# A two-layer network with two recurrences and two mixtures of experts: the first mixture taken out of the first recurrence

## What is computed

```python
x = x + linear_attention(local_attention(x, cond))      # 16 heads of 64
x = x + ffn0(gru(cond, x))
x = x + diff_attention(gated_recurrence(cond, x))
x = x + ffn1(modulate(x, cond))
```

```python
def step(h, inp):                      # h is [8, 128]
    r = sigmoid(xr_t + h @ W_hr)
    z = sigmoid(xz_t + h @ W_hz)
    n = tanh(xn_t + r * (h @ W_hn + b_hn))
    return (1.0 - z) * n + z * h
```

```python
for e in range(8):
    y = relu(tokens @ W1[e] + b1[e]) @ W2[e] + b2[e]     # 128 -> 512 -> 128
    out = out + where(final_e == e, y, 0.0)
```

## Time and profile before

| | us |
|---|---|
| median of three runs | 1699.1 (1698.83 to 1703.48) |
| the profiled execution | 1703.39, its span 1701.6 |
| PE busy | 1564.6 (92% of the span), 11861 passes |
| DVE, ACT, POOL busy | 827.5, 662.9, 94.7 |

### The profile page before, as it was taken

One profiled execution on the slowest core, in us unless ns is written; L12 is line 12 of the kernel. 1 busy time (PEld: TensorE's weight loads), 2 busy tenths in 40 slices (PEclk: granted clock), 3 DMA queues, 4 the chain that ended last, 5 costly groups with the idle time before them and its releaser, 6 DMA issues. The chain is left out here.

```text
span 1701.6 us, 32009 instructions
## 1 busy us (share of the span) xinstructions
PE 1564.6 (92%) x11861; PEld 1250.0 (73%) x11862; DVE 827.5 (49%) x2926; ACT 662.9 (39%) x2449; POOL 94.7 (6%) x135
## 2 busy tenths in 40 slices
PE   7999989879999899999999999879999999866995
PEld 5666555537777799999999999638888888753663
DVE  2777668755445334444444444473333333565223
ACT  3211112125555145555555455314344434523442
POOL 0000000000000000000000000010000000003662
PEclk9988889889999999999999999859999999967998
DMA  4000000000000300000000000010000000001113
GB/s 146 1 1 1 0 1 1 1 0 1 1 1 1 100 1 2 2 1 2 2 2 1 2 2 1 1 31 21 20 26 20 27 14 2 1 1 47 41 43 92
DMA packets 27731, 28.05 MB, mean 16 GB/s; under 512 B 2293, under 2 KB 22234, under 8 KB 27450
## 3 DMA queue, kind: packets, MB, share of 16 engines
q1 hardware_dynamic: 20970, 16.70, 3.4%
q0 software_dynamic: 2496, 5.12, 1.0%
q10 hardware_dynamic: 4112, 4.19, 0.8%
HBM read 21.35 MB, written 4.65 MB: 15 GB/s over the span
## 5 line engine op out<-in xcount | busy, mean ns | idle before, releaser
L1457 PE MATMUL spare<-identb 128*128 128x128 bf16 x3166 | 218.2, 219 | 0.0
L1457 PEld LDWEIGHTS spare<-identb 128*128 128x128 bf16 x3166 | 201.7, 103 | 4.3
L292 PE MATMUL sc<-headsel,prod 128*128 128x128 f32 x1024 | 164.6, 315 | 0.7 <-DVE prod L437 0.7
L292 PEld LDWEIGHTS sc<-headsel,prod 128*128 128x128 f32 x1024 | 142.6, 218 | 26.7 <-issue 24.3
L1055 DVE TENSOR_TENSOR_SCAN narg<-rz,pre_n 128x16 f32<-128x16 f32 x256 | 47.9, 187 | 219.9 <-PE pre_n L952 218.9
L990 ACT ACTIVATE ghid<-gh_ps,cols 128x128 f32<-128x128 f32 x512 | 144.3, 366 | 12.9 <-PE gh_ps L891 12.7
L891 PE MATMUL gh_ps<-hist,w 128*128 128x128 f32 x1024 | 137.5, 275 | 0.6 <-ACT ghid L990 0.6
L900 PE MATMUL gy_ps<-w2e,ghid 128*128 128x128 f32 x1024 | 136.8, 276 | 0.6
L900 PEld LDWEIGHTS gy_ps<-w2e,ghid 128*128 128x128 f32 x1024 | 124.4, 191 | 3.0 <-issue 3.0
L891 PEld LDWEIGHTS gh_ps<-hist,w 128*128 128x128 f32 x1024 | 126.0, 188 | 0.8 <-DVE hist L1063 0.8
L952 PE MATMUL pre_r<-hist,gru_w 128*128 128x128 f32 x512 | 118.1, 312 | 0.7 <-DVE hist L1063 0.5
(11 more groups left out here) (374 smaller groups left out, 2664.1 us busy)
## 6 DMA issues: line engine op xcount, KB each, us to landing
w<-in_L_ffn_W SPq DMA_DIRECT2D x1, 2048.0 KB, 9.6
raw<-in_L_ffn_wg SPq DMA_DIRECT2D x8, 256.0 KB, 2.9
raw<-in_L_ffn_wu SPq DMA_DIRECT2D x8, 256.0 KB, 2.8
raw<-in_L_ffn_wd SPq DMA_DIRECT2D x8, 256.0 KB, 2.7
wqkv<-in_L_attn_Wqkv SPq DMA_DIRECT2D x1, 1536.0 KB, 6.4
mrow<-mt SPq DMA_DIRECT2D x4, 256.0 KB, 2.4
y_top<-yrow SPq DMA_DIRECT2D x4, 256.0 KB, 5.4
y_next<-yrow ACTq DMA_DIRECT2D x4, 256.0 KB, 6.1
```

Source lines behind the costliest of these rows:

```text
L292: mm = nc.tensor.matmul(sc[:, :, :, :].rearrange("p i j h -> p (i j h)"), prod[u % 2][:, j, P * i:P * i + P], headsel[:, P - 2 * k:2 * P - ...
L1457: nc.tensor.matmul(spare[:, 0:P], n.identb[:, :], n.identb[:, :], start=True, stop=True)
```

## The change

In gru_scan the mixture's jobs, diff, y0, choice and the hist clearing go. The three products of a step stream the eight columns of the state. At step 3 of a group PE turns the group's 128 states (one transposition), ACT copies them to htok, and SP stores them as rows of a DRAM tensor hrow. Fills stand in every step: 12, or 8 where input products are fed, and both now come behind them. b1 and b2 are loaded to all partitions by SP. In route_top1 the diagonal and the adding go; chosen and kept stay for a new stage, sparse_ffn: final expert (one), places and lists as in sparse_experts with 16 pair columns and 24 block columns, then 23 slots, each with a gather, one hidden product, and bias adds on VectorE; rows are scattered to frow, read back in four parts by SP, turned, and added to xT.

```diff
-    FILL = 16
+    FILL = 12
+    INPUT_FILL = 8
+    RING = 4
...
+                sp.dma_start(b1B[:, :], a["L0_ffn_b1"].rearrange("(r e) f -> r (e f)", r=1).broadcast_to([P, E * FF])).then_inc(n.load_experts, 16)
+                sp.dma_start(b2B[:, :], a["L0_ffn_b2"].rearrange("(r e) d -> r (e d)", r=1).broadcast_to([P, E * D])).then_inc(n.load_experts, 16)
+                for g in range(GROUPS):
+                    sp.wait_ge(h_kept, g + 1)
+                    sp.dma_start(hrow[P * g:P * g + P, :], htok[g % RING][:, :]).then_inc(h_stored[g % RING], 16)
...
-            @block.gpsimd
-            def _(pool):
-                pool.memset(hist[:, 16 * 40:], 0.0).then_inc(hist_zero, 1)
...
+                for s in range(T):
+                    h = second(at_step(s))
+                    pe.wait_ge(state, s + 1)
+                    for out, i, ready in ((gate_slot(pre_r, s), 3, r_pre), (first(n_slot(s)), 5, n_pre), (gate_slot(pre_z, s), 4, z_pre)):
+                        nc.tensor.matmul(out, n.gru_w[:, i, :], h, start=False, stop=True,
+                                         skip_group_check=True).then_inc(ready, 1)
+                    if s >= G and s % G == TURN_AT:
+                        turn(s // G - 1)
                     g, i = s // G + 1, s % G - 9
-                    if g < GROUPS and 0 <= i < 7:
+                    feeds = g < GROUPS and 0 <= i < 7
+                    if feeds:
                         inputs(g, i)
+                    for _ in range(INPUT_FILL if feeds else FILL):
+                        nc.tensor.matmul(spare[:, :], n.identb[:, :], n.identb[:, :], start=True, stop=True)
+                pe.wait_ge(state, T + 1)
+                turn(GROUPS - 1)
+                for k in range(NBLK):
+                    b, half = divmod(k, SEG)
+                    states = hist[:, 16:16 * (T + 1)].rearrange("p (t b two) -> p two b t", b=B, two=2)[:, 1]
+                    mm = nc.tensor.matmul(pre_r[0][:, E * k:E * k + E], states[:, b, P * half:P * half + P],
+                                          n.cols[:, r0:r0 + E], start=True, stop=True)
+                mm.then_inc(all_logits, 1)
...
+def sparse_ffn(nc, n, chosen, kept, hrow, frow, w1, w2, b1B, b2B):
+
+    SLOTS = (TOK + E * (P - 1)) // P
+    COLS = 24
+    AHEAD = 8
+    RING = 10
+    YRING = 4
...
+                def hidden(j):
+                    if j >= SLOTS:
+                        return
+                    at[j] = pe.value_load(owner_i[0:1, j:j + 1], min_val=0, max_val=E - 1)
+                    pe.wait_ge(x_kept, j + 1)
+                    if j >= 2:
+                        pe.wait_ge(hid_done, j - 1)
+                    nc.tensor.matmul(h_ps[j % 2][:, :], xT[j % 3][:, :],
+                                     w1[:, bass.ds(at[j], 1), :].rearrange("p e f -> p (e f)"),
+                                     start=True, stop=True).then_inc(h_in, 1)
...
+                def down(j):
+                    pe.wait_ge(t_kept, j + 1)
+                    if j >= 1:
+                        pe.wait_ge(y_kept, j)
...
+                for j in range(SLOTS):
+                    hidden(j + 1)
+                    turn_in(j + 2)
+                    turn_hidden(j)
+                    if j >= 1:
+                        down(j - 1)
+                down(SLOTS - 1)
+                pe.wait_ge(t_kept, SLOTS)
+                for g in range(4):
+                    pe.wait_ge(f_back[g], 16)
...
+                for j in range(SLOTS):
+                    keep_in(j + 2)
+                    act.wait_ge(t_in, j + 1)
...
+                    nc.scalar.activation(hidT[j % 2][:, :, :], t_ps[j % 2][:, :, :], ACT.Relu).then_inc(t_kept, 1)
...
+                def add(j):
...
+                    own[j] = dve.value_load(owner_i[0:1, j:j + 1], min_val=0, max_val=E - 1)
+                    dve.wait_ge(h_in, j + 1)
+                    if j >= 2:
+                        dve.wait_ge(t_in, j - 1)
+                    V.tensor_tensor(hid[j % 2][:, :], h_ps[j % 2][:, :], b1B[:, bass.ds(own[j] * FF, FF)], ALU.add).then_inc(hid_done, 1)
+
+                def keep_out(j):
+                    dve.wait_ge(y_in, j + 1)
+                    if j >= YRING:
+                        dve.wait_ge(scattered[j % YRING], 16 * (j // YRING))
+                    V.tensor_tensor(ysb[j % YRING][:, :], y_ps[:, :], b2B[:, bass.ds(own[j] * D, D)], ALU.add).then_inc(y_kept, 1)
...
+                for j in range(SLOTS):
+                    gather(j + AHEAD)
+                    pool.wait_ge(y_kept, j + 1)
+                    pool.indirect_dma_start(out=frow[:, :],
...
+                for g in range(4):
+                    sp.dma_start(back[:, 4 * g:4 * g + 4, :],
+                                 frow[512 * g:512 * g + 512, :].rearrange("(i p) d -> p i d", p=P)).then_inc(f_back[g], 16)
```

More of the change, by code:

```diff
@@ L884, in inputs @@
                     nc.tensor.matmul(out, lhsT, rhs, start=(i < 3), stop=False, skip_group_check=True)
[L886 to L932, removed]
-                    if k == 7 and g < GROUPS:
-                        pe.wait_ge(choice_kept, g + 1)
-                        nc.tensor.matmul(turn_ps, n.b2[:, :], choiceT[:, :], start=True, stop=True).then_inc(bias_in, 1)
@@ L1119, in route_top1 @@
         counts = sb("r_counts", [P, 3, NBLK])
-        rank, kept = sb("r_rank", [P, NBLK]), sb("r_kept", [P, NBLK])
-        diag = sb("r_diag", [P, NBLK, P], BF16)
-        added = [sb(f"r_added{i}", [P, 2 * T]) for i in range(4)]
+        rank = sb("r_rank", [P, NBLK])
         const = sem("r_const"); step = sem("r_step")
@@ L1304, in _ @@
             def _(pe):
[L1305 to L1315 removed]
+                pe.wait_ge(const, 2)
@@ new lines, in _ @@
+                pe.wait_ge(taken_done, 1)
+                nc.tensor.matmul(tot_ps, ones[:, :], taken[:, :, :], start=True, stop=True)
+                nc.tensor.matmul(cum_ps, tri[:, :], taken[:, :, :], start=True, stop=True).then_inc(counted, 1)
+                pe.wait_ge(pay_done, 2)
+                for q in range(NBLK):
+                    if q % 8 == 0:
+                        pe.wait_ge(lane_done, q // 8 + 1)
+                    mm = nc.tensor.matmul(inv_ps[:, :], in_lane[:, q, :], load[:, q, :, :].rearrange("p k c -> p (k c)"),
+                                          start=(q == 0), stop=(q == NBLK - 1), skip_group_check=True)
@@ new lines, in _ @@
+                at = {}
+                pe.wait_ge(owners, 1)
+                turn_in(0)
+                turn_in(1)
+                hidden(0)
+                for j in range(SLOTS):
+                    hidden(j + 1)
+                    turn_in(j + 2)
+                    turn_hidden(j)
+                    if j >= 1:
+                        down(j - 1)
[3 more added lines that the diff above has]
+                    pe.wait_ge(f_back[g], 16)
+                    if g >= 2:
+                        pe.wait_ge(added, g - 1)
+                    for i in range(4):
+                        mm = nc.tensor.transpose(t_ps[g % 2][:, i, :], back[:, 4 * g + i, :], n.ident[:, :])
+                    mm.then_inc(turned, 1)
@@ new lines, in done, with after, per_token @@
+                def done(ins):
+                    at[0] += 1
+                    ins.then_inc(step, 1)
+                def after():
+                    dve.wait_ge(step, at[0])
+                def per_token(ap):
+                    return ap.unsqueeze(2).broadcast_to(wide)
+                done(V.tensor_scalar(dropped[:, :], kept[:, :], -1.0, 1.0, ALU.mult, ALU.add))
+                done(V.tensor_tensor(one[:, :, :], chosen[:, :, :], per_token(kept[:, :]), ALU.mult))
+                after()
@@ new lines, in _ @@
+                dve.wait_ge(blk_done, 1)
+                V.tensor_tensor(load[:, :, 1, :], in_blk[:, :, :], pair_no[:, :].unsqueeze(2).broadcast_to(every),
+                                ALU.mult).then_inc(pay_done, 1)
+                for c in range(2):
+                    eight = [P, 8, P]
+                    V.tensor_tensor(in_lane[:, 8 * c:8 * c + 8, :], lane[:, :].unsqueeze(1).broadcast_to(eight),
+                                    lo_f[:, 8 * c:8 * c + 8].unsqueeze(2).broadcast_to(eight), ALU.is_equal).then_inc(lane_done, 1)
```

434 lines of the change are left out of this document (259 added, 175 removed).

## The result

The changed kernel takes 1940.8 us (median of 4 runs, 1937.7 to 1952.3), the kernel before 1699.0 beside it: ratio 1.144, 95% interval 1.138 to 1.150. The forecast was 1690. The profiled execution has a span of 1939.0 us and a mean granted clock of 0.779, against 1701.6 and 0.942 before.

What follows compares the result with a forecast made beforehand. It took the state-to-state chain to bound steps without extras, TensorE's queue the others. Terms -3.4, -65.5, -17.4 and +77 (new stage) sum to -9.3 us: 1703.4 profiled to 1694.1, as median 1690; own range 1681 to 1699.

Steps and rivals of the forecast that it cites:

- rival 3: Recurrence: with fewer columns streamed the clock falls, 2.7 us a step at the lower level, 1715 to 1780 us; chance 0.05.
- recurrence: First recurrence, 256 steps: falls from 485.7 to 420.2 us, -65.5 us, mean step 1.65 us.
- Narrow products: Recurrence steps without extras: eight columns instead of 128 take 0.11 us off, 1.72 to 1.61 us.
- Rival 1: Recurrence: narrow products save less; 0.05 us instead of 0.11 gives 1705 us, nothing gives 1718; chance 0.16.
- bias steps: Recurrence steps 12 to 15 of a group, feeding a one-row bias: bound by TensorE's queue at 1.76 us.
- Start: Before the recurrence: hist memsets and two VectorE constants go, products start earlier; -3.4 us.
- Behind the recurrence: Between recurrence and ranking: mixture jobs and router products shrink to 32 router passes, 26.1 to 8.7 us, -17.4 us.
- Lists: Beginning of the new stage: building the lists on VectorE up to the first gather takes 13.0 us.
- filling: New stage after the lists: first gather to first hidden product takes 5.0 us.
- Slots: New stage, 23 slots: each takes 2.30 us, with GpSimd's 2.58 us a transfer pair covered by gathering eight ahead.
- Rival 2: New stage: slots stall as TensorE waits for the copied output; 3.16 us a slot gives 1709 us; chance 0.16.
- The last part: End of the new stage, after the last output product: read-back, transposes, last add and block change, 12.0 us.

Runs made afterwards that it cites:

- e18: Changed kernel with only the middle product (n) streaming 128 columns again, fills 12 and 8, one-row biases; 1694.1 us (ratio 0.9976).
- e2: Changed kernel with fills where input products are fed raised from 8 to 12, so all steps have twelve; 1991.7 us (ratio 1.168).
- e7: Kernel before the change with its three products narrowed from 128 to 8 columns, mixture jobs and sixteen fills kept; 2086.8 us (ratio 1.228).
- e11: e9 with one pause: in step 64 VectorE first fills a tile of 8192 columns; 1953.7 us, a single run.
- e9: Changed kernel with fifteen and twelve fills and biases fed by weights of 128 rows instead of one; 1695.6 us (ratio 0.9973).
- e6: Changed kernel with fills raised to twenty, and sixteen in steps 9 to 15; 2145.1 us (ratio 1.253).
- e10: e9 with all 23 gathers issued ahead of the first scatter, 23 input and 12 output buffers; 1707.3 us (ratio 1.004).

## Why the prediction was wrong

- **The clock, rival 3 at 0.05.** This is the step that failed: the sum took the full clock for the whole recurrence. Its term was 420.2 us, and 656.7 was measured, 236.5 of the 250.8 us between forecast and median. Against the rival stood: "Against it: the second recurrence, eight columns with fourteen fills a step, ran at 0.99". The comparison was made per step. A step of the second recurrence lasts 1.19 us and has one product, so fourteen fills in 1.19 us; here twelve stand in 1.60 us beside six passes of eight columns, where six passes of 128 columns stood before. That this difference of the two steps is the reason is argued and not shown, since no run varies it alone; what is shown is that the same fills hold the clock when one of the three products is wide (e18). The rival's price per step, 2.7 us, was right (42.1 / 16 = 2.63 measured); that the fall would be for the whole recurrence was not in its prices, 1715 to 1780, since I took it for granted that the clock comes back. The kernel after itself, e2, e7 and e11 show that it does not. The row quoted for a falling clock, "two stretches with idle TensorE at 0.50", has one stretch at 0.50 in the earlier trace rows; the ranking, which is not among these rows, has 0.54.
- **Narrow products, -0.11 us a step.** Right: 1.60 measured, 1.61 forecast. Rival 1 is out. The bias steps were priced too high, 1.76 for 1.60 in step 12: the one-row load starts 0.77 us into the step and not 0.84 (591.48 against 590.71), the fills' loads come 0.41 later, as priced, and the next product's load 0.42 behind their start, not 0.45 and 0.05. A single weight load of 0.19, from which the six passes were priced, is not in the earlier trace rows, which show the pair alone; loads of this length stand elsewhere in the trace. Where the clock holds, the recurrence takes 411.7 to 413.1 us; forecast 420.2. The Trainium skill, TensorE: Matmul & The Clock Gate, Single matmul latency, made 0.05 us of the same columns; the readers of this trace moved by 0.11. The Trainium skill gives that formula for a single bf16 product, and these are float32 products of two passes.
- **Start, -3.4.** Measured -5.0 to the first state.
- **Behind the recurrence, -17.4.** Measured -18.0, at half the clock: 32 router passes take 6.92 us, as priced.
- **Lists 13.0 and filling 5.0.** Measured 13.0 and 5.1.
- **Slots 2.30 us.** Wrong for the first fifteen, 3.0 on average. From the first gather to the end of the last output product it takes 73.4 us (1287.85 to 1361.21) for 60.2, so 13 us more. Rival 2's price (3.16 a slot) is near, its place is not: the product is finished by the profile and its readers start late, while gathers go out. The last part, from there to the end of the stage, took 11.3 for 12.0. The prediction had weighed GpSimd's 2.58 us for a pair as a matter of its queue only.
- **The sum.** e18, where the clock holds, takes 1694.1 against 1690 forecast, inside the range; by its profiled span, 1693.0, it is -5.5 at the start, -73.8 in the recurrence, -18.3 behind it, +89.1 in the stage. Against the terms, -3.4, -65.5, -17.4 and +77, that is 8.3 less in the recurrence and 12.1 more in the stage, so part of this nearness is luck: two errors cancel. And what all terms stood on, an unchanged clock, was not tested by them.

## What to carry to other kernels

Before a product that streams more columns than it needs is made narrow, ask what the clock will do: here the narrowing saved 0.11 us a step and, with the fills as they were, cost the full clock. That another stage held its clock with fills of about this number proves little when its steps are shorter and hold other passes. If the latency of one product is hidden, as n's here, leave that one wide. And try a kernel that is paced by such a chain with one short pause: if the clock does not come back by itself, a gain of some tenths of a per cent stands on a trap of 250 us.

## What the runs showed that was not expected

TensorE at 1.2 GHz can be busy in 636.40 of 636.40 us and not be given 2.4 again. The Trainium skill, TensorE: Matmul & The Clock Gate, section What's actually happening, says that the clock is throttled by default and that activity releases it; to be busy by the profile is not enough by these runs. Whether a step keeps its level also depends on which level it is at: fifteen and twelve fills held the clock in ten runs of e9 and could not bring it back in e11. Fills alone rank oddly against a product: e6, with sixteen to twenty fills and narrow products, fell, and e18, with eight to twelve and one wide product, held. Why a wide pass does more than a fill of as many columns is open; the runs do not separate number format, data and place in the queue. And beside the gathers, readers of products that had ended by the profile started 12 to 20 us late in e10, on VectorE and on ScalarE, with no wait in the program to explain it.
